# A twelve-sublayer decoder kernel: statistics of x in the stage tails, the output bias on GpSimd, the result stored batch by batch, and no spare identity products on TensorE

## The reference

```python
def _layernorm(x, axis=-1, eps=1e-05):
    m = jnp.mean(x, axis=axis, keepdims=True)
    v = jnp.var(x, axis=axis, keepdims=True)
    return (x - m) / jnp.sqrt(v + eps)
...
x = x + _L0_attn_ref(_layernorm(x, axis=-1), ...)
x = x + _L0_xattn_ref(_layernorm(x, axis=-1), ctx_1024, ...)
x = x + _L0_ffn_ref(_layernorm(x, axis=-1), ...)
...
x = x + _L3_ffn_ref(_layernorm(x, axis=-1), ...)
```

```python
q, k, v = x @ Wq + bq, ctx @ Wk + bk, ctx @ Wv + bv      # 16 heads of 16
attn = softmax(q @ k.T / 4)
out = (attn @ v) @ Wo + bo
```

## Time and profile before

| What | us |
|---|---|
| Runs of the kernel | 1487.43, 1482.93, 1479.32; median 1482.93 |
| The profiled execution | 1481.45 |
| its span on the core | 1479.7 |
| PE busy | 1352.3 (91%) |
| DVE busy | 781.0 (53%) |
| ACT busy | 647.5 (44%) |
| POOL busy | 194.7 (13%) |

### The profile page before, as it was taken

How to read it: one execution, slowest core, us unless ns; L and a number is a source line. 1 busy time by engine, 2 the same in 40 slices (tenths; PEclk the granted TensorE clock), 3 DMA queues, 4 the chain that set the end, 5 groups by cost and what they waited for, 6 DMA issues and landing times. The chain is left out here.

```text
span 1479.7 us, 31590 instructions
## 1 busy us (share of the span) xinstructions
PE 1352.3 (91%) x12492; PEld 1050.6 (71%) x12492; DVE 781.0 (53%) x1773; ACT 647.5 (44%) x1685; POOL 194.7 (13%) x201
## 2 busy tenths in 40 slices
PE   7999899989989899999999978999997896799887
PEld 6776668866557678777999965679984575588632
DVE  3666677755556677620000277711138485576765
ACT  3443326643357446434444345533225674266300
POOL 3000160000014400040111420041112000300000
PEclk9999999999999999999999989989998997999999
DMA  6000132011311100166999200274311000610100
GB/s 219 1 1 1 50 64 43 4 44 36 76 19 22 32 24 4 38 216 239 344 346 346 61 5 23 71 308 159 142 61 37 1 2 1 110 14 4 68 1 22
DMA packets 44125, 120.57 MB, mean 81 GB/s; under 512 B 12011, under 2 KB 28521, under 8 KB 38593
## 3 DMA queue, kind: packets, MB, share of 16 engines
q1 hardware_dynamic: 33228, 62.40, 14.6%
q0 software_dynamic: 7616, 53.14, 10.4%
q10 hardware_dynamic: 3136, 3.03, 0.7%
HBM read 96.13 MB, written 11.02 MB: 72 GB/s over the span
## 5 line engine op out<-in xcount | busy, mean ns | idle before, releaser
L826 PE MATMUL wide<-early_kt,early_q 32*100 32x361 f32 x512 | 95.4, 484 | 2.8 <-PEq L66 1.6
L2555 ACT ACTIVATE l1f_hidden<-wide,l1f_pack 128x128 f32<-128x128 f32 x160 | 58.7, 367 | 78.1 <-PE wide L2494 68.2
L2677 DVE TENSOR_TENSOR l1f_out<-summed,l1f_pack 128x256 f32<-128x256 f32 x20 | 8.5, 425 | 152.7 <-PE summed L2502 152.7
L2494 PEld LDWEIGHTS wide<-l1f_rt,l1f_pack 128*128 128x128 f32 x640 | 74.5, 192 | 1.8 <-issue 0.8
L2494 PE MATMUL wide<-l1f_rt,l1f_pack 128*128 128x128 f32 x640 | 74.8, 275 | 0.6 <-ACT l1f_rt L2545 0.6
L2502 PE MATMUL summed<-l1f_pack,l1f_hidden 128*128 128x256 f32 x320 | 72.4, 379 | 0.0
L2502 PEld LDWEIGHTS summed<-l1f_pack,l1f_hidden 128*128 128x128 f32 x320 | 59.2, 190 | 7.2
L3770 PE MATMUL wide<-l3f_we,l3f_xt 128*100 128x512 f32 x128 | 59.8, 622 | 1.2 <-DVE l3f_acc L3838 1.2
L1220 DVE TENSOR_REDUCE l3x_mx<-wide 100x2 f32<-100x722 f32 x64 | 55.2, 903 | 3.0 <-PE wide L826 3.0
L1220 DVE TENSOR_REDUCE l1x_mx<-wide 100x2 f32<-100x722 f32 x64 | 55.2, 903 | 2.8 <-PE wide L826 2.8
L1220 DVE TENSOR_REDUCE l0x_mx<-wide 100x2 f32<-100x722 f32 x64 | 55.2, 903 | 1.8 <-PE wide L826 1.8
(11 more groups left out here) (626 smaller groups left out, 3370.1 us busy)
## 6 DMA issues: line engine op xcount, KB each, us to landing
l2f_w<-l2f_w_dram SPq DMA_DIRECT2D x16, 1024.0 KB, 12.0
ctxt<-ctxt_dram SPq DMA_DIRECT2D x4, 1083.0 KB, 17.3
early_kt<-soon_kd SPq DMA_DIRECT2D x32, 90.8 KB, 3.2
l1f_sorted_x<-l1f_zeros SPq DMA_DIRECT2D x4, 640.0 KB
l1f_rows<-l1f_sorted_x SPq DMA_DIRECT2D x20, 128.0 KB, 7.4
l1f_sorted_y<-l1f_out ACTq DMA_DIRECT2D x20, 128.0 KB, 9.0
l0f_w<-l0f_w_dram SPq DMA_DIRECT2D x18, 128.0 KB, 2.1
l1f_shared<-l1f_shared_dram SPq DMA_DIRECT2D x1, 2180.0 KB, 10.3
```

Of the source, the lines that this page charges most:

```text
L826: pe.matmul(wide[0:S, i, 0:SKV], q4[R * i:R * (i + 1), g % 2, b, g // 2, :], kt[R * i:R * (i + 1), g % 2, b, g // 2, 0:SKV], start=True, s ...
L2494: last = pe.matmul(wide[:, f % 4, 0:P], w1_of(w, k, f), rt[:, n % 2, k, :], start=k == 0, stop=k == KC - 1)
L2555: act.activation(hidden[:, f, 0:P], wide[:, f % 4, 0:P], ACT.Gelu, bias=b1_of(pack[:, n % SLOTS, :], f)).then_inc(sem["h_ready"], 1)
L2677: dve.tensor_tensor(out[:, n % 2], summed[:, n % 2, 0:E], b2_of(pack[:, n % SLOTS, :]), ALU.add).then_inc(sem["y_ready"], 1)
```

## The change

Five things change.

1. `keep_busy` and all its calls are gone.
2. The statistics of x move from the heads of l0f, l1f, l2f, l3x and l3f into the tails of the sublayers before them (l0x, l1x, l2x, l3a, l3x). The tail takes `bn_stats` batch by batch as x is finished, then the aggregation, the root (with its table loaded beforehand on ACT) and the reciprocal. l0x keeps its own head statistics.
3. In `cross_attn16` POOL adds the output bias to x, one batch at a time, before the loop's results come; DVE then adds the product straight from its bank to x. The number of DVE instructions per batch is unchanged: an addition and a `bn_stats` where two additions were.
4. In l2f the scatter of `none`, the last row's numbers and `spot` come before the last expert's output.
5. In l3a POOL clears `v` in seven pieces behind the normalisation and adds the bias batch by batch. In l3f each batch of x is stored as soon as it is finished; the store block is gone.

```diff
-def keep_busy(pe, net, count):
-    for _ in range(count):
-        pe.matmul(net.summed[:, 1, 0:P], net.ident[:], net.ident[:], start=True, stop=True)
+def rstd_vector(dve, net, var_ready, std_ready, count):
+    dve.tensor_scalar(net.std[:], net.moments[:, :, 1:2], EPS, None, ALU.add).then_inc(var_ready, 1)
+    dve.wait_ge(std_ready, count)
+    dve.reciprocal(net.rstd[:], net.std[:])
+    dve.drain()
...
 # cross_attn16, PE
-                if not spread:
-                    keep_busy(pe, net, 18 if fresh else 12)
...
                 score(0, 1)
-                if fresh:
-                    keep_busy(pe, net, 5)
-                else:
+                if not fresh:
                     values(B - 1)
...
                         weigh(n - 2)
-                    if n == 0:
-                        keep_busy(pe, net, 3)
 # cross_attn16, ACT, at its end
+                act.preload_act_table(ACT.Sqrt)
+                act.wait_ge(sem["var_ready"], STATED)
+                act.activation(net.std[:], net.std[:], ACT.Sqrt).then_inc(sem["std_ready"], 1)
 # cross_attn16, POOL, at its end
+                pool.wait_ge(sem["wo_loaded"], 32)
+                if not spread:
+                    pool.wait_ge(sem["xn_ready"], B)
+                for b in range(B):
+                    pool.tensor_tensor(net.x[:, b, :], net.x[:, b, :], bo[:], ALU.add).then_inc(sem["x_ready"], 1)
 # cross_attn16, DVE, at its end
-                    if b >= 3 and bo is not None:
-                        add_bias(b - 3)
+                    if b >= 3:
+                        add(b - 3)
                     dve.drain()
                     if b < B:
                         divide(b)
                     if b >= 3:
-                        add(b - 3)
-                dve.drain()
+                        dve.bn_stats(net.stats[:, b - 3, :], net.x[:, b - 3, :])
+                    if b == B + 1:
+                        dve.drain()
+                        for one in range(B - 1):
+                            dve.bn_aggr(net.moments[:, one, :], net.stats[:, one, :])
+                dve.drain()
+                dve.bn_aggr(net.moments[:, B - 1, :], net.stats[:, B - 1, :])
+                dve.drain()
+                rstd_vector(dve, net, sem["var_ready"], sem["std_ready"], STATED)
...
 # l2_ffn, POOL
                 for e in range(FIN):
+                    if e == FIN - 1:
+                        pool.wait_ge(sem["about_ready"], NE)
+                        scatter(FIN, lambda c: none[:], sem["none_stored"])
                     pool.wait_ge(sem["y_ready"], e + 1)
                     scatter(e, lambda c: out[:, e % 2, c, :], stored[e % 2])
-                pool.wait_ge(sem["about_ready"], NE)
-                scatter(FIN, lambda c: none[:], sem["none_stored"])
...
 # l3_attn, POOL
-                pool.memset(v[:], 0.0).then_inc(sem["cleared"], 1)
-                pool.wait_ge(sem["bo_loaded"], 16)
-                pool.wait_ge(sem["xn_ready"], T)
-                pool.tensor_tensor(net.x[:], net.x[:], bo[:].unsqueeze(1).broadcast_to([S, T, E]), ALU.add).then_inc(sem["x_ready"], 1)
+                pool.wait_ge(sem["xn_ready"], T)
+                for n in range(NB):
+                    last = pool.memset(v[:, n], 0.0)
+                last.then_inc(sem["cleared"], 1)
+                pool.wait_ge(sem["bo_loaded"], 16)
+                for t in range(T):
+                    pool.tensor_tensor(net.x[:, t, :], net.x[:, t, :], bo[:], ALU.add).then_inc(sem["x_ready"], 1)
...
 # l3_ffn, SP
+                for b in range(B):
+                    sp.wait_ge(sem["x_done"], b + 1)
+                    sp.dma_start(dram["out"][b], net.x[:, b, :]).then_inc(sem["stored"], 16)
+                sp.wait_ge(sem["stored"], 16 * B)
```

More of the change, by code:

```diff
@@ L270, in heads @@
         return self.v1[0:self.rows_of(c), b, c, 0:16 * 17].rearrange("s (h w) -> s h w", w=17)[:, :, 0:16]
[L273 to L280, removed]
 @sublayer
@@ L1470, in _ @@
                 copy_yt(B - 1)
+                act.preload_act_table(ACT.Sqrt)
+                act.wait_ge(sem["var_ready"], 2)
+                act.activation(net.std[:], net.std[:], ACT.Sqrt).then_inc(sem["std_ready"], 1)
             @block.gpsimd
@@ L1520, in _ @@
                         add(u // 2 - 2)
+                    if u >= 6 and u % 2 == 0:
+                        dve.bn_stats(net.stats[:, u // 2 - 3, :], net.x[:, u // 2 - 3, :])
                 for b in range(B - 2, B):
+                    dve.drain()
+                    dve.bn_stats(net.stats[:, b - 1, :], net.x[:, b - 1, :])
+                    if b == B - 1:
+                        dve.drain()
+                        for one in range(B - 1):
+                            dve.bn_aggr(net.moments[:, one, :], net.stats[:, one, :])
                     add(b)
                 dve.drain()
+                dve.bn_stats(net.stats[:, B - 1, :], net.x[:, B - 1, :])
+                dve.drain()
+                dve.bn_aggr(net.moments[:, B - 1, :], net.stats[:, B - 1, :])
+                dve.drain()
+                rstd_vector(dve, net, sem["var_ready"], sem["std_ready"], 2)
 def top_two_vector(dve, net, t, gap_ready, exp_ready, both=None, both_ready=None):
@@ L3207, in _ @@
                     learn(e)
+                    if e == FIN - 1:
+                        learn(FIN)
+                        dve.drain()
+                        for c in range(RT):
+                            dve.tensor_scalar(spot[:, c, :], numbers[:], about[:, FIN, c, 2:3], about[:, FIN, c, 0:1],
+                                              ALU.is_equal, ALU.mult).then_inc(sem["spot_ready"], 1)
                     dve.wait_ge(sem["y_psum"], e + 1)
@@ L3215, in _ @@
                     last.then_inc(sem["y_ready"], 1)
-                learn(FIN)
-                dve.drain()
-                for c in range(RT):
-                    dve.tensor_scalar(spot[:, c, :], numbers[:], about[:, FIN, c, 2:3], about[:, FIN, c, 0:1],
-                                      ALU.is_equal, ALU.mult).then_inc(sem["spot_ready"], 1)
                 for n in range(PARTS):
@@ L3697, in _ @@
                         keep_shares(n - 1)
-                dve.wait_ge(sem["x_ready"], 1)
+                dve.wait_ge(sem["x_ready"], T)
                 for t in range(T):
+                    if t == T - 1:
+                        for one in range(T - 2):
+                            dve.bn_aggr(net.moments[:, one, :], net.stats[:, one, :])
                     dve.wait_ge(sem["out_psum"], t + 1)
                     dve.tensor_tensor(net.x[:, t, :], net.x[:, t, :], wide[0:S, t % 4, 0:E], ALU.add).then_inc(sem["out_done"], 1)
+                    if t >= 1:
+                        dve.bn_stats(net.stats[:, t - 1, :], net.x[:, t - 1, :])
+                    dve.drain()
+                dve.bn_stats(net.stats[:, T - 1, :], net.x[:, T - 1, :])
                 dve.drain()
+                for one in range(T - 2, T):
+                    dve.bn_aggr(net.moments[:, one, :], net.stats[:, one, :])
+                dve.drain()
+                rstd_vector(dve, net, sem["var_ready"], sem["std_ready"], 1)
 @sublayer
@@ L3781, in _ @@
             def _(act):
-                norm_stats_scalar(act, net, sem["var_ready"], sem["std_ready"])
+                act.preload_act_table(ACT.Exp)
                 def copy_xt(b, slot, first):
@@ L3845, in choose @@
                     dve.drain()
-                    dve.tensor_tensor(net.x[:, b, :], net.x[:, b, :], one, ALU.add)
+                    dve.tensor_tensor(net.x[:, b, :], net.x[:, b, :], one, ALU.add).then_inc(sem["x_done"], 1)
                 by_pairs(dve, B, choose)
@@ L3923, in build @@
         l3_ffn(net)
-        store(net)
 def front(net):
```

59 lines of the change are left out of this document (22 added, 37 removed).

## The result

The changed kernel took 1492.35 us (median of 14 runs, 1487.09 to 1498.40) against 1485.38 for the kernel before (14 runs): a ratio of 1.0051, 95% interval 1.0031 to 1.0071, some 7.5 us slower. I had forecast 1478, no measurable change. The time lies inside the range given, on the other side of the kernel before; the prediction had given a time above 1490.3 a chance of 0.23.

What follows compares the result with a forecast made beforehand. TensorE (PE), busy nearly throughout, was taken as the bound; -3.5 - 2.5 - 2.5 - 1.9 + 0 + 7.2 = -3.2 from the profiled 1481.45 gave 1478 us, range 1468 to 1495.

Steps and rivals of the forecast that it cites:

- Spare products, +7.2: Removing keep_busy: loop heads gain 1.0; cold clock costs 6.8 in l1x and l3x, 0.7 each in l0x loop and head.
- my 6.8: Loop starts of l1x and l3x together: cost in us of a stretch of 6.83 us at half clock in each.
- Statistics, -1.9: Statistics moved from five heads into preceding tails: shorter heads less longer tails and cold starts, net 1.9 us gained.
- l3x (-1.85): Boundary l3a to l3x: whole head gain of 4.25 us shows, less longer tail and projections at 1.2 GHz, net -1.85.
- l3f (-0.6): Boundary l3x to l3f: 1.6 of the head's 4.25 us taken because the weight load limits the logits, net -0.6.
- Store, -3.5: Program's end: storing by batches cuts SyncE's 5.8 us wait towards that of a small transfer, gaining 3.5 us.
- End of l2f, -2.5: Scatters of none ahead of the last expert's output let the gathered tokens come earlier, gaining 2.5 us.
- Head of l3a, -2.5: Starting POOL's memset of v later removes one normalisation of 3187 ns that the transposes wait for, gaining 2.5 us.
- Bias on GpSimd, 0: Three cross_attn16 stages: POOL's bias additions, 17.4 us together, fit into DVE's idle time and cost nothing.
- The rival of the lock: POOL's additions lock DVE in the loops: from +12 (1490) up to +17.4 (1495); chance 0.10.
- The loop that stays cold: Clock falls and stays down in l1x or l3x quads: 1540 for one loop, 1601 for two; chance 0.15.
- The case without any price of the clock: Clock doesn't fall at loop starts, or its fall hides behind DVE's first maxima: 1470 us; chance 0.20.

## Why the prediction was wrong, step by step

- **Spare products, +7.2: this is the step that failed.** Left out alone they cost 19 us (14 to 24). The mechanism was right where I looked: the clock fell in the loops of l1x and l3x and came back, and a cold quad took 1.86 us more than a warm one where I had taken 2.1. From the first scores to the last addition the changed kernel lost 2.7 us in l1x and 4.0 in l3x, 6.7 for my 6.8 (in l3x the kernel before has a pause of 1.35 us that the changed one hasn't, so the clock took some 5.4 there). What I left out was the rest of the kernel. l2x is not in the sum at all, and lost 7 us in both profiled kernels without any product. The l0x loop, in the sum at +0.7, lost 4.2 us in the changed kernel and 3.2 with the products alone left out; some 2 us of that is a pause (last section) and not the clock. The cold heads I priced in l0f, at +1.0, and in l3x, at +0.5. Between the profile of before and that with the products alone left out, l0f's first expert work lost 1.7 us more than the end of l0x, l2f's 1.3. I had read the products as work in PE's waits, and asked only where it delays something. How the 19 us divide among the stages isn't settled by one trace a kernel: l0a, which no run changes, differs by 3.3 us between profiled executions.
- **Statistics, -1.9.** With products, the move and the bias cost 0.0067, some 10 us; without, the rest of the change leaves 7.6 - 19 + 10.2 = -1.2 for them, by difference of three ratios and so uncertain by some 7 us. Within that, l1f and l2f went as argued: the loads took the head's gain. l3x (-1.85) failed: the normalisations met POOL's memset, 5.01 us for 2.68, and from the last addition of l3a to the first scores it took 21.44 us, 1.6 longer than before; with the loops' products back it was the 19.85 of before, no gain either. l3f (-0.6) failed too: I took 1.6 of gain, but the logits wait for all of the block's loads, and came 0.7 us later behind l3x's last addition (12.34 for 11.63).
- **Store, -3.5: right, and larger.** From the last addition to the span's end it is 1495.0 - 1492.2 = 2.8 us, before 1479.7 - 1472.3 = 7.4: -4.6.
- **End of l2f, -2.5: right**, -2.3. **Head of l3a, -2.5:** the long normalisation went, but only 1.5 us reached the keys' products. Together the three were measured at -10.2, where I had -8.5.
- **Bias on GpSimd, 0: right.** The maxima kept their 903 ns beside the additions. The rival of the lock is out for the loops. The Trainium skill, SBUF — State Buffer, section "SBUF: two separate sides", has the lock only for some forms of DVE instruction; the maxima here agree with being none of them, and the normalisations of 5.01 us beside a memset with being one.
- **The rivals.** The loop that stays cold didn't come: the longest stretch was 17.07 us. The lock in the loops didn't come either. The range reached up to 1495 for its sake alone, so that 1492.35 lies inside is luck. The case without any price of the clock is out. The Trainium skill, TensorE: Matmul & The Clock Gate, section "What's actually happening", takes the throttled state as the default; the trace agrees (0.50 for some 185 us where it was 104), and the rule would have sent me to ask at every place where a product stood, not in the loops alone.

How firmly is the clock the cause? In single runs of one kernel, time and clock go together: the changed kernel's runs lie from 1487.09 us at a clock of 0.941 to 1498.40 at 0.932. Counting (1 - clock) x 2 x span as cold time, a line through all 141 runs of the changed kernel and the twelve of the experiments, each about its own mean, gives 0.34 us per cold microsecond. That is a correlation over runs. What shows that the products are the cause is the run with them alone left out; that they act through the clock rests on the stretches at 0.50 and the units in them that take nearly twice as long. A product at a place is no guarantee in either direction: l1x's loop fell once with its products, and l2x's stood once without.

## What to carry to other kernels

Work that nothing reads can still be load-bearing: before it is removed, list every place where it stands, and price at each what the clock does to the work behind it, not only what it delays. Moving work out of a head is worth only what the next waiting thing leaves, here loads, and a memset or a filler that was harmless beside it will stand in the open. When one edit carries five parts, measure the parts alone: three of these were worth 0.7%, and were hidden by a fourth.

## What the runs showed of the hardware that I had not expected

In a loop of small tiles the clock stayed at 0.50 for 13.65 us (l2x, 917.47:931.12) although PE was busy for 13.46 of them, while the same loop stood at 1.00 throughout in the run with only the other loops' products back. Being busy again did not bring the clock back at once, and none of these runs shows what did.

PE stood still in the middle of a row of products that wait for nothing (time line of l0x's loop, changed kernel):

```profile
233.34 0.53 PE L842 MATMUL summed<-l0x_pt,l0x_v 121*32 121x100 f32 x11
236.95 0.54 PE L842 MATMUL summed<-l0x_pt,l0x_v 121*32 121x100 f32 x13 [3.07 <-issue]
```

In that time, by the table of queues from 233.9 to 236.9 us (packets, MB, share), one packet of instructions came:

```profile
q8 instruction: 1, 0.02, 2.9%
```

The pause was 2.09 us in the same loop where the products alone were left out, and in the kernel before a pause of 1.35 us stood in l3x's loop at the same products. That it is a late load of instructions fits, and isn't shown: 98 such packets came in this execution, and nearly all without a pause. It makes some 2 us of the l0x loop's loss, and these aren't the clock's.
